# First norm written over the residual rows, its scale and shift moved in the GpSimd order, epsilon on GpSimd, one unit off VectorE

## What is computed

```python
for l in range(L):                                   # L = 2, d = 192, FF = 768
    a = _longformer_attn(x, ...)                     # softmax over [global, band]
    x = _ln(x + a, g1[l], beta1[l])                  # first norm:  (x-m)*rsqrt(v+1e-5)*g + b
    h = jax.nn.relu(x @ W1[l].T + b1[l]) @ W2[l].T + b2[l]
    x = _ln(x + h, g2[l], beta2[l])                  # second norm
```

## Time and profile before

| | us |
|---|---|
| median of 3 runs (lowest, highest) | 882.41 (881.75, 885.37) |
| profiled execution, whole / span of its instructions | 888.34 / 886.6 |
| PE busy, share of the span | 795.6 (90%) |
| DVE / ACT / POOL busy | 630.5 / 559.0 / 558.0 |
| mean granted clock of TensorE | 0.975 |

### The profile page before, as it was taken

How to read it: one execution, slowest core, us unless ns; L and a number is a source line. 1 busy time by engine, 2 the same in 40 slices (tenths; PEclk the granted TensorE clock), 3 DMA queues, 4 the chain that set the end, 5 groups by cost and what they waited for, 6 DMA issues and landing times.

```text
span 886.6 us, 23620 instructions
## 1 busy us (share of the span) xinstructions
PE 795.6 (90%) x8467; PEld 609.2 (69%) x8467; DVE 630.5 (71%) x1903; ACT 559.0 (63%) x1558; POOL 558.0 (63%) x820
## 2 busy tenths in 40 slices
PE   6989998999999989989999989999999899886496
PEld 3767766667777666667777657677775568775495
DVE  4899956447999664568997453789993765987553
ACT  4878884348788853267888642678887434465364
POOL 5558876543488765364888563527886754767354
PEclk9999999999999999999999999999999999998699
DMA  2300010512000003230000006100000060501330
GB/s 77 110 7 4 3 34 23 175 34 79 3 4 3 23 26 122 86 97 24 4 3 3 23 19 185 54 31 4 3 4 2 1 203 1 215 1 61 97 106 22
DMA packets 38659, 43.84 MB, mean 49 GB/s; under 512 B 7226, under 2 KB 33945, under 8 KB 38409
## 3 DMA queue, kind: packets, MB, share of 16 engines
q1 hardware_dynamic: 18124, 19.30, 7.4%
q10 hardware_dynamic: 18148, 18.29, 6.7%
q0 software_dynamic: 2272, 4.74, 1.7%
HBM read 20.70 MB, written 21.59 MB: 48 GB/s over the span
## 4 chain that ended last, share of the span: by engine, by line
PE 60%; DVE 21%; POOL 7%; issue 6%; ACT 3%; DMA 1%; POOLq 0%; SPq 0%; DVEq 0%; ACTq 0%
PE bank L1420 7%; DVE p L1132 6%; PE bank L1593 5%; DVE nmx L1123 5%; PE bank L1666 4%; PE bank L1642 4%; PE bank L1718 4%; PE bank L1717 4%; PE bank L1529 4%; PE bank L1541 3%; PE bank L1596 3%; POOL p L609 3%; PE bank L1756 2%; PE bank L1645 2%; PE bank L1765 2%
## 5 line engine op out<-in xcount | busy, mean ns | idle before, releaser
L609 POOL TENSOR_TENSOR p<-p 128x384 f16<-128x384 f32 (+1 forms) x320 | 282.7, 904 | 93.8 <-ACT p L808 89.3
L806 ACT ACTIVATE p<-bank 128x384 f32<-128x384 f32 (+1 forms) x384 | 170.2, 451 | 49.5 <-PE bank L1645 32.4
L1123 DVE TENSOR_REDUCE nmx<-bank 128x1 f32<-128x384 f32 (+1 forms) x384 | 190.3, 511 | 13.9 <-PE bank L1596 9.5
L1642 PE MATMUL bank<-stack 103*128 103x128 bf16 x1056 | 143.0, 220 | 2.5 <-ACT p L808 1.6
L808 ACT ACTIVATE p<-bank 128x384 f16<-128x384 f32 (+1 forms) x320 | 144.3, 451 | 0.0
L1645 PE MATMUL bank<-bandb,idb 128*128 128x128 bf16 x672 | 134.2, 220 | 0.0
L1666 PE MATMUL bank<-vst,p 128*128 128x49 bf16 x2112 | 116.2, 185 | 12.4 <-DVE p L1132 9.6
L1593 PE MATMUL bank<-stack 100*128 100x384 bf16 (+1 forms) x384 | 120.3, 313 | 7.2 <-DVE nmx L1123 2.9
L1666 PEld LDWEIGHTS bank<-vst,p 128*128 128x128 f16 x2112 | 89.2, 96 | 30.0 <-DVE p L1132 15.5
L1642 PEld LDWEIGHTS bank<-stack 103*128 103x128 bf16 x1056 | 87.3, 98 | 24.4 <-issue 15.1
L1596 PE MATMUL bank<-bandb,idb 128*128 128x128 bf16 x672 | 100.5, 219 | 0.0
(11 more groups left out here) (247 smaller groups left out, 1786.8 us busy)
## 6 DMA issues: line engine op xcount, KB each, us to landing
xs<-zrow ACTq DMA_DIRECT2D x8, 2193.0 KB, 12.5
xt<-xs SPq DMA_DIRECT2D x23, 129.0 KB
w2s<-in_w SPq DMA_DIRECT2D x4, 576.0 KB
mwbs<-in_mwb SPq DMA_DIRECT2D x1, 2064.0 KB, 8.6
mw2s<-in_mw SPq DMA_DIRECT2D x1, 2048.0 KB, 12.9
lnrow<-in_lnr SPq DMA_DIRECT2D x4, 480.0 KB
stack<-mtr SPq DMA_DIRECT2D x96, 3.0 KB
w1b<-in_w SPq DMA_DIRECT2D x4, 291.0 KB
```

Of the source, the lines that this page charges most:

```text
L609: nc.gpsimd.tensor_tensor(p2[:, u % RING, 0:w], p32[:, u % RING, 0:w], p1[:, u % RING, 0:w], ALU.subtract).then_inc(p2_pool, 1)
L806: ins = nc.scalar.activation(p32[:, s % RING, 0:w], ps[2 + s % 3][:, 0:w], ACT.Exp)
L1123: nc.vector.tensor_reduce(nmx[:, vn % 3, h:h + 1], nat_bank(v)[:, 0:w], AX.X, ALU.max, negate=True).then_inc(max_done, 1)
L1642: ins = mm(ps[2 + s % 3][:, blk(i)], stack[0:K_ALL, H + h, blk(m)], stack[0:K_ALL, h, blk(n)], start=True, stop=m == n)
```

## The change

The diff cut to its core. `KEPT` says at which entries of the list GpSimd makes the `resid` of the first norm. No other engine looks at it.

```diff
+def on_dve(u):
+    return u % SHARE == SHARE - 1 and u < U - 1
+def dve_units(u):
+    return sum(on_dve(i) for i in range(u))
...
             def rstd_of(j):                                           # GpSimd
                 pool.wait_ge(y_stats, at(y_stats, j + 1))
+                ch.link(nc.gpsimd.tensor_scalar(ve[:, j % 4:j % 4 + 1], mv[:, j % 4, 1:2], EPS, None, ALU.add))
                 nc.gpsimd.tensor_tensor(rstd[...], ve[...], colc[:, 3:4], ALU.pow).then_inc(y_rstd, 1)
...
             def residual(b, j):
                 k, n = j // NB, b * NB + block_of(j)
-                pool.wait_ge(z_ready, at(z_ready, j + 1))
-                ch.link(nc.gpsimd.tensor_tensor(resid[:, n, :], zt[:, j % 4, :], lnrow[:, 2 * k, :], ALU.mult))
+                z = resid[:, n, :]
+                if k == 0:
+                    pool.wait_ge(z_mm, at(z_mm, j + 1))
+                else:
+                    pool.wait_ge(z_ready, at(z_ready, j + 1))
+                    z = zt[:, j % 4, :]
+                ch.link(nc.gpsimd.tensor_tensor(resid[:, n, :], z, lnrow[:, 2 * k, :], ALU.mult))
...
-                        if 0 <= u < U and u % SHARE != SHARE - 1:     # GpSimd, p2
+                        if 0 <= u < U and not on_dve(u):
...
+                        for i in KEPT.get((kind, j), ()):
+                            residual(b, i)
-                        if kind == "z":
+                        if kind == "z" and j >= NB:
                             residual(b, j)
...
-                            nc.scalar.activation(ata[:, 0:1], ps[2][0:DLO, 0:1], ACT.Copy)      # oc, ScalarE
+                            nc.scalar.activation(ata[:, 0:1], ps[3][0:DLO, 0:1], ACT.Copy)
-                            if s % SHARE != SHARE - 1:                # ScalarE, p1
+                            if not on_dve(s):
...
             def stats(j, src):                                        # VectorE
                 ch.link(nc.vector.bn_stats(stt_[:, j % 4, :], src))
-                ch.link(nc.vector.bn_aggr(mv[:, j % 4, :], stt_[:, j % 4, :]))
-                nc.vector.tensor_scalar(ve[...], mv[:, j % 4, 1:2], EPS, None, ALU.add).then_inc(y_stats, 1)
+                nc.vector.bn_aggr(mv[:, j % 4, :], stt_[:, j % 4, :]).then_inc(y_stats, 1)
             def normed(j, src, dst):
+                dve.wait_ge(y_stats, at(y_stats, j + 1))
                 dve.wait_ge(y_rstd, at(y_rstd, j + 1))
...
+                        if s == U + 3:                                # VectorE, in step(s)
+                            dve.wait_ge(gathered, 16 * NB * (b + 1))
+                            dve.wait_ge(y_mm, at(y_mm, 1))
+                            y = y_bank(0, False)
+                            ch.link(nc.vector.tensor_tensor(y, y, resid[:, b * NB + block_of(0), :], ALU.add))
+                            stats(0, y)
...
-                        if 0 <= u < U and u % SHARE == SHARE - 1:     # VectorE, cast and p2
+                        if 0 <= u < U and on_dve(u):
...
-                    dve.wait_ge(gathered, 16 * NB * (b + 1))
-                        if kind == "y":
+                        if kind == "y" and i:
                             dve.wait_ge(y_mm, at(y_mm, i + 1))
...
                         if kind == "z":
-                            if i >= 4:
+                            if i >= NB + 4:
                                 dve.wait_ge(z_mm, ...)                # buffer zt free again
                                 dve.wait_ge(resid_ready, ...)
-                            normed(i, y, zt[:, i % 4, :]).then_inc(z_ready, 1)
+                            z = zt[:, i % 4, :] if i >= NB else resid[:, b * NB + block_of(i), :]
+                            normed(i, y, z).then_inc(z_ready, 1)
...
-                    nc.tensor.transpose(bank[0:DLO, 0:P], zt[:, zc % 4, 0:DLO], idf[:, :])
-                    ins = nc.tensor.transpose(bank[0:DHI, P:2 * P], zt[:, zc % 4, DLO:D], idf[:, :])
+                    z = zt[:, zc % 4, :] if zc >= NB else resid[:, (rnd // L) * NB + block_of(zc), :]
+                    nc.tensor.transpose(bank[0:DLO, 0:P], z[:, 0:DLO], idf[:, :])
+                    ins = nc.tensor.transpose(bank[0:DHI, P:2 * P], z[:, DLO:D], idf[:, :])
...
                         if s == U + 4:                                # TensorE, in step(s)
                             pe.wait_ge(exp_done, at(exp_done, U))
+                            y_block(2)
                             pe.wait_ge(f_norm, at(f_norm, 1))
-                                mm(ps[2][0:DLO, 0:1], og[:, i, 0:DLO], fst[:, 0:1], ...)       # oc
+                                mm(ps[3][0:DLO, 0:1], og[:, i, 0:DLO], fst[:, 0:1], ...)
...
-                        if kind == "y" and i >= 2:
-                            if i == 2:
-                                pe.wait_ge(oc_copied, at(oc_copied, 1))
+                        if kind == "y" and i >= 3:
                             y_block(i)
...
+KEPT = {("hid", 0): (0,), ("hid", 1): (1,), ("hid", 2): (2, 3), ("tr", 4): (4,), ("tr", 5): (5,), ("tr", 6): (6,),
+        ("tr", 7): (7,)}
```

More of the change, by code:

```diff
@@ L383, in program @@
             (U, (nat_mm, max_done, t_mm, exp_done, pv_mm)),
-            (U - U // SHARE, (p2_pool,)),
-            (U // SHARE, (p2_dve,)),
+            (U - dve_units(U), (p2_pool,)),
+            (dve_units(U), (p2_dve,)),
             (2 * (FF // P), (h_mm, h_relu)),
@@ L513, in _ @@
                     if l == L - 1 and b + 1 < B:
-                        sp.wait_ge(p2_pool, at(p2_pool, U - U // SHARE))
-                        sp.wait_ge(p2_dve, at(p2_dve, U // SHARE))
+                        sp.wait_ge(p2_pool, at(p2_pool, U - dve_units(U)))
+                        sp.wait_ge(p2_dve, at(p2_dve, dve_units(U)))
                         load_ids(b + 1)
@@ L782, in step @@
                             act.wait_ge(oc_mm, at(oc_mm, 1))
-                            nc.scalar.activation(ata[:, 0:1], ps[2][0:DLO, 0:1], ACT.Copy)
-                            nc.scalar.activation(atb[0:DHI, 0:1], ps[2][0:DHI, 8:9], ACT.Copy).then_inc(oc_copied, 1)
+                            nc.scalar.activation(ata[:, 0:1], ps[3][0:DLO, 0:1], ACT.Copy)
+                            nc.scalar.activation(atb[0:DHI, 0:1], ps[3][0:DHI, 8:9], ACT.Copy).then_inc(oc_copied, 1)
                         n, o = divmod(s + H, H)
@@ L960, in stats @@
                 ch.link(nc.vector.bn_stats(stt_[:, j % 4, :], src))
-                ch.link(nc.vector.bn_aggr(mv[:, j % 4, :], stt_[:, j % 4, :]))
-                nc.vector.tensor_scalar(ve[:, j % 4:j % 4 + 1], mv[:, j % 4, 1:2], EPS, None, ALU.add).then_inc(y_stats, 1)
+                nc.vector.bn_aggr(mv[:, j % 4, :], stt_[:, j % 4, :]).then_inc(y_stats, 1)
             def normed(j, src, dst):
+                dve.wait_ge(y_stats, at(y_stats, j + 1))
                 dve.wait_ge(y_rstd, at(y_rstd, j + 1))
@@ L1567, in step @@
                             pe.wait_ge(exp_done, at(exp_done, U))
+                            y_block(2)
                             pe.wait_ge(f_norm, at(f_norm, 1))
                             for i in range(3):
-                                mm(ps[2][0:DLO, 0:1], og[:, i, 0:DLO], fst[:, 0:1], start=i == 0, stop=i == 2)
+                                mm(ps[3][0:DLO, 0:1], og[:, i, 0:DLO], fst[:, 0:1], start=i == 0, stop=i == 2)
                             for i in range(3):
-                                ins = mm(ps[2][0:DHI, 8:9], og[:, i, DLO:D], fst[:, 0:1], start=i == 0, stop=i == 2)
+                                ins = mm(ps[3][0:DHI, 8:9], og[:, i, DLO:D], fst[:, 0:1], start=i == 0, stop=i == 2)
                             ins.then_inc(oc_mm, 1)
@@ L1654, in step @@
                                 pe.wait_ge(comb, at(comb, 2 * (n - 1) + g + 1))
-                            if w % SHARE == SHARE - 1:
-                                pe.wait_ge(p2_dve, at(p2_dve, w // SHARE + 1))
+                            if on_dve(w):
+                                pe.wait_ge(p2_dve, at(p2_dve, dve_units(w + 1)))
                             else:
-                                pe.wait_ge(p2_pool, at(p2_pool, w + 1 - w // SHARE))
+                                pe.wait_ge(p2_pool, at(p2_pool, w + 1 - dve_units(w)))
                             if i == 0:
```

## The result

| | before | after |
|---|---|---|
| median of 8 executions each (lowest, highest) | 882.59 (881.40, 885.37) | 875.31 (872.82, 878.13) |
| profiled execution, whole / span | 888.34 / 886.6 | 877.06 / 875.3 |
| mean granted clock of TensorE over all timed executions | 0.970 to 0.973 (the four groups of runs below) | 0.974 |

The ratio is 0.991, 95% interval 0.9892 to 0.9929: faster by 7.3 us between the medians, by 7.9 by the ratio. One execution of before (2567.28 us) and one of e4 (1255.72 us), both in the runs of the experiments and far above all others, are left out of every median and ratio. The forecast was 8.8 us less, 873.6, with a range of 871.0 to 877.8. The two profiled executions lie 11.3 us apart, because the one of before happened to spend 3.7 us more in the expert part behind the last y15 (128.3 against 124.6 us).

The account below looks back on a forecast made before the run. TensorE was taken as the bound, waiting for VectorE ahead of hid 0: 7.36 us over four rounds, less 0.27 at round ends, plus 1.43 and 0.29 in round 3, took 8.8 off 882.41, giving 873.6 us, range 871.0 to 877.8.

Parts of the forecast that it names:

- TensorE bound by VectorE ahead of hid 0, y0 early, epsilon off VectorE: Last combination to hid 0: 1.08 us from y0's early add plus 0.76 from the epsilon, 1.84 us a round.
- This needs unit 95 off VectorE; the two edits have one price: End of attention: y0's add fits ahead of the combination only with unit 95 off VectorE; together 1.08 us a round.
- t = 0.28: Assumed time in us of GpSimd's epsilon add with the wait on itself; hidden up to 0.43, costing 0.09 at round ends.
- `resid` moved is the condition of the rest: First norm: GpSimd's latency stays hidden only without `resid` between powers; before, a block cost GpSimd 1.73 us, VectorE 1.46.
- The rival on the slower side: Norm blocks: at an add of 1.5 us the chain VectorE to GpSimd and back sets every block; 886.7 us, chance 0.05.
- Round 3, hid 4's stall: Round 3: GpSimd reaches `stream(0)` earlier without `resid` ahead, so the wait before hid 4 goes; 1.43 us gained.
- rival A: Round 3: GpSimd's `resid` runs late, so y8's norm and all behind slip 2 to 3 us; 876.1 us, chance 0.13.
- In the two stretches behind that ... 0.29 us: Round 3, y10 to y11 and y14 to y15: one VectorE epsilon goes at each, 2 x 0.19 less 0.09 at z15.
- the rule weighed: VectorE and GpSimd share an exclusively locked port pair, the loser blocking for the whole instruction; moved GpSimd instructions could stretch.
- y2 ahead of the global token: Before hid 0: y2's two passes, 0.66 us, ahead of `oc` cost nothing, with 0.5 us of cover for y3.
- rival D: Round starts: longer pauses lose TensorE's clock, some 1.4 us each, 876.4; or a round 3 dip goes, 871.9; chance 0.07.
- rival E: Round 0 before hid 0: a single late start or pause of GpSimd leaves 4.4 of 8.8 us; 878.0 us, chance 0.03.

Follow-up runs that it names:

- e4: The changed kernel with the first norm written to `zt` and its `resid` instructions back between GpSimd's powers: 885.16 us, ratio to before 1.005.
- e1: The changed kernel with the epsilon add back on VectorE in both norms: 875.58 us, ratio to before 0.9927.
- e3: The changed kernel with y0's add and statistics back behind all steps: 879.75 us, ratio to before 0.9973.
- e2: The changed kernel with unit 95's cast and remainder back on VectorE, y0's add still early: 875.72 us, ratio to before 0.9931.
- e9: The changed kernel itself, unedited, timed again on another chip: 879.82 us, ratio to before 0.9922.
- e10: The changed kernel with the second norm's epsilon back on VectorE, the first norm's still on GpSimd: 873.08 us, ratio to before 0.9851.
- e8: The changed kernel with y2's product again behind the global token's products: 877.44 us, ratio to before 0.9914.
- e12: The same kernel as e10, timed again on another chip: 874.92 us, ratio to before 0.9882.

## Why the forecast came out

- **TensorE bound by VectorE ahead of hid 0, y0 early, epsilon off VectorE: right.** Forecast 1.84 us a round, measured 1.86, and block by block 1.27. Its parts were off against each other: the epsilon 1.06 instead of 0.76, since it costs VectorE 0.22 us a block and not 0.19, and also delays y0's statistics ahead of the combination by 0.18 (e1), and the rest 0.80 instead of 1.08 (before against e1). Each grows if the other is made (e3: 1.16 with both). That the sum agrees to 0.02 us is in part luck.
- **"This needs unit 95 off VectorE; the two edits have one price": right in kind.** 0.40 us a round of it hangs on unit 95 (e2), and not all.
- **t = 0.28: right,** measured 0.30, 0.22 for the add and 0.08 to its power, and the hand-over from VectorE is 0.09 (329.22 to 329.31) where I took 0.08. At round ends, where the latency counts, it costs 0.14 and not 0.09: 0.42 us instead of 0.27.
- **`resid` moved is the condition of the rest: right,** and e4 shows its size, 8.3 us. The 1.73 us a block on GpSimd that the forecast put against VectorE's 1.46 became 2.07 with the epsilon there. The rival on the slower side (VectorE to GpSimd and back sets every block) is what e4 shows, reached through the queue and not through the price of the add.
- **Round 3, hid 4's stall: right,** 1.43 us as forecast. GpSimd's late `resid` did stay within y8's cover (rival A false): all 32 multiplications of the first norm's `resid` took 579 to 602 ns. Of the 32 additions one took 0.73 us and one, in round 1, 1.52:

```profile
335.86 1.52 POOL L604 TENSOR_TENSOR resid<-resid,lnrow 128x192 f32<-128x192 f32 x1
```

It stands beside the same comparison of VectorE as the 1.55 us of before. So the trace agrees with the rule of the Trainium skill, SBUF — State Buffer, "two separate sides", at the new place too. There the stretching cost nothing, since TensorE covers it: hid 0 to `mv` 8 is 14.83 us in rounds 0 to 2, before and after. In the second norm VectorE's instructions grew, as the next point shows.

- **"In the two stretches behind that ... 0.29 us": this step failed.** Forecast -0.38 us between `mv` 8 and `mv` 15, measured +0.45: 0.83 us off, in three places.

The first two are the ones I had counted. `mv` 10 to `mv` 11 is 3.70 us in e9 and 3.56 before, in e1 and in e10; `mv` 14 to `mv` 15 is 5.05 in e9 and 4.90 before and in e1. I booked the 0.19 us of VectorE's instruction that goes, at each. It does go, but other instructions of VectorE grow. GpSimd's power and `resid` instructions now come later behind `mv`, VectorE's own instructions earlier, and VectorE's L1023 (L1005 before) runs while GpSimd multiplies. One row of before, then three of e9:

```profile
722.29 0.17 DVE L1005 TENSOR_SCALAR vin<-mean 128x2 f32<-128x2 f32 x1
```
```profile
711.64 0.59 POOL L603 TENSOR_TENSOR resid<-zt,lnrow 128x192 f32<-128x192 f32 x1
711.87 0.38 DVE L1023 TENSOR_SCALAR vin<-mean 128x2 f32<-128x2 f32 x1
712.23 0.78 DVE L1044 TENSOR_SCALAR z<-resid,mean,rs 128x192 f32<-128x192 f32 x1
```

L1023 lasts 0.38 instead of 0.17 us, and 0.51 instead of 0.21 at the second place; the z behind the first lasts 0.78 instead of 0.62. In e10, with the second norm's epsilon on VectorE, the first two last 0.17 and 0.65 us. So the place of the epsilon sets when the two meet. In e3, with the epsilon on GpSimd, the second meeting came out the other way: the z lasted 0.36 us, the next z 0.61 instead of 0.34, GpSimd's addition 0.73 instead of 0.59, and `mv` 10 to `mv` 11 stayed at 3.56. That it is the exclusion of the rule weighed is argued from the overlap alone, and was not tested by itself.

The third, `mv` 11 to `mv` 12, I had not counted. Here VectorE has no other block to work on, and what counts is the latency from `mv` to z: for block 11 it is 1.25 us in e9 (714.23 to 715.48), 1.13 before (724.27 to 725.40) and 1.10 in e10. The whole stretch is 21.58 us in e4 and 21.42 in e1, neither with a clock drop: +0.16. Together that is 0.14 + 0.15 + 0.16 = 0.45 us.

- **y2 ahead of the global token "cost nothing": right** at full clock (0.05 us a round in e8).
- **The clock (rival D):** I put it at the pauses of round starts, +-1.4 to 1.7 us. On one chip the mean clock was 0.972 before and 0.974 after (e9), a difference within their scatter (single executions go from 0.968 to 0.977). But in e10 and e12, with one epsilon left on VectorE, it is 0.978. Single drops at round starts came and went as the rival has it: one in the profile of before, two in the first of the changed kernel, one in e9. The late first call (rival E) did not appear: all 64 adds on GpSimd took 212 to 232 ns, and hid 0 of round 0 came 9.46 us after the last exponential as in the other rounds.

By stretches the gain is 8.0 us, of 8.9 forecast for the same stretches: +0.08 ahead of hid 0, -0.15 at round ends, -0.83 in round 3. The medians moved by 7.3 us and the ratio says 7.9, with an interval of about 1.6 us to either side, so the total alone would not have told which term was off.

## What to carry to other kernels

Take a small instruction off the engine that is the bound, and put it where its latency is hidden; keep it where the next block can't start before it comes back. First clear the queue of the engine that takes it: here that was worth more than the move. And see what its other instructions then stand beside: here two of VectorE's grew by about 0.2 us each when the two engines had shifted by 0.1 to 0.2 us against each other. Look at the mean granted clock over all executions before you credit or blame an edit for a few microseconds of the total; the timeline between two fixed events tells 0.4 us where the total does not tell 2.

## What the runs showed that I had not expected

- A kernel's granted clock moves with edits of 0.1 to 0.3 us: 0.978 with the second norm's epsilon on VectorE, on three chips (e1, e10, e12), against 0.974 in the changed kernel, while its single drops fall in other places in each execution. The row of one, in the changed kernel, with TensorE at half clock (0.50, 1.2 of 2.4 GHz) and busy throughout, right behind the pause of 1.81 us:

```profile
718.98:725.80 6.82, 6.82 (x21) 4.69 (x21) 2.98 (x11) 2.02 (x5) 3.79 (x7) 0.50 0.00 0
```

- An add over a 128x1 column costs GpSimd 0.22 us (212 to 232 ns, 64 of them) and VectorE 0.15.
- Chips differ by more than some edits do: before had medians of 882.5, 883.4, 885.9 and 884.8 us on four of them.
